# Edge loops of two graph layers: longer loop bodies, one comparison of a block reused for the next, and a comparison in fp32

## The chip, the cores and the metric

The kernel runs on one core of a Trainium2 chip. The metric is the device time of one execution in microseconds (us). TensorE (PE in the rows, PEld its weight loads) multiplies matrices, VectorE (DVE), ScalarE (ACT) and GpSimd (POOL) do the rest, and SyncE (SP) issues loads.

## What is computed

Four graph layers run one behind the other over 6250 nodes with 64 features and 206250 edges (100000 random pairs both ways, and a loop at each node), sorted by the destination `dst`. Each layer gathers something for the source of each edge and sums it per destination:

```python
edge_index = jnp.stack([src, dst])
x = layernorm(x + layer0(x, ...))   # two weighted sums over edges
x = layernorm(x + layer1(...))      # sum and maximum of edge features
x = layernorm(x + layer2(...))      # 4 Gaussian kernels: agg += segment_sum(gw[:, k] * xt[src, k], dst)
x = layernorm(x + layer3(...))      # messages: relu([x[src], x[dst], edge] @ W1.T + b1) @ W2.T + b2,
                                    # segment_sum(messages, dst), then a GRU cell
```

The change touches the loops over edges of layers 2 and 3.

## The kernel before

**Blocks.** The edges are cut into 51 blocks of 4096 (`NBK`), which are placed once, ahead of the layers, in a grid of 49 tiles of 128 node slots (`NT`), so that most edges of a block stand at the place of their source node. The rest of them, 9 x 128 rows of a block (`SC` = 9), is kept as a second list. A block's destinations lie in a window of 128 (`W`) nodes, those of its second list in groups of columns of 160 (`WS`). How many groups of columns a block may need is counted at run time (`n_windows`); for these inputs it is one, and there is one round over the blocks.

**How a sum is made.** The scatter to destinations is a matmul with a one-hot matrix: VectorE compares a row of numbers 0, 1, 2, ... with each edge's relative destination, and TensorE multiplies. A block takes 7 parts (`NS`) of 7 tiles (`SUB`), one comparison of 128 x 896 elements each (`g_hot` in layer 2, L2003; `m_hot` in layer 3, L2579). The second list has one-hots of its own, 128 x 9 x 160 in fp32 (`onehot`, made by `expand`, L2007 and L2600).

**Layer 2** (`layer2_edges`, L1880 on). For each part TensorE does 42 matmuls in bf16 (L1954), then a small one that turns a tile (L1961, once a block), at the end of the block 18 matmuls in fp32 for each group of columns (L1967, 36 instructions in the trace). VectorE makes for block n the products of the second list (L2019) and its one-hots, then in `hots` the comparisons for block n + 1, each as soon as TensorE has used that buffer, then it adds the block's window to the accumulators (L2034) and in the loop over groups of columns the second window (L2041), and expands again. GpSimd issues 9 gathers for a block (L1934), which wait for TensorE's progress (`hot_used`) so that they are spread over the block before.

**Layer 3** (`layer3_edges`, L2311 on). TensorE turns the edge features (L2429, L2430), makes the products of a part (L2439, L2443; ready: `pre_ready`), and three parts later reduces it (`reduce`, L2457 and L2460). In between, VectorE adds the source part (`add_src`, L2584), and with ScalarE splits the result into three bf16 parts (`take_high` L2590, `take_middle` L2596, after which `reduce` may start: `lo_ready`). At u == 1 VectorE also does `second`: cast the second list's destinations (L2606), subtract the group's first column (L2609), expand (L2600). At u == 5 it makes `mark` (L2620). At the block's end, in a loop over the groups of columns, it subtracts 160 from `rel` (L2665), waits for TensorE's window (L2508), adds it (L2667) and expands again, whether another group follows or not:

```python
with dve.Fori(0, count) as w:
    col = dve.value_load(cols[0:1, bass.ds(w, 1)], min_val=0, max_val=z.NP)
    v.tensor_scalar(rel[:, :], rel[:, :], -float(WS), None, ALU.add)
    dve.wait_ge(win_ready, before + w + 1)
    v.tensor_tensor(k.acc0[0:D, bass.ds(col, WS)], win_s[:, :], k.acc0[0:D, bass.ds(col, WS)], ALU.add)
    dve.drain()
    expand()
```

Then it adds the block's window (L2671), which sets `fast_ready`, and counts up `free`, after which SyncE loads for three blocks on. GpSimd issues 18 gathers a block in 9 pairs (L2407 and L2410, `m_from_src` and `m_from_dst`), of which six pairs first wait for a product of the block before (`pre_ready`).

**The loops.** Every engine runs the blocks through `over_rounds` (L656). Its body is written out for 6 blocks (two triples, since the buffers go by threes), and the loop turns 8 times; the last three blocks stand in line behind it.

## Time and profile before

| | |
|---|---|
| plain executions, median of 3 | 8629.86 us (8614.71 to 8640.16) |
| profiled execution | 8661.29 us, its span 8658.9 us |
| TensorE, weight loads | busy 60% and 50% of the span |
| VectorE | busy 53% |
| GpSimd | busy 50% |
| ScalarE | busy 18% |
| TensorE's granted clock over the span | 0.76 of full speed |

The profile shows one execution. The edge loop of layer 2 lies between about 5140 and 6545 us from the span's start, that of layer 3 between 6745 and 8575 us. In a row of a timeline stand start, duration, engine, line, operation, what it writes and reads, shapes and how many were merged; in square brackets how long the engine had been idle before it and what ended that ("issue": nothing that the profile shows; "remote": a semaphore whose setter it doesn't name). A name such as "DMA grid<-pay_d" as a releaser can stand for another use of the same semaphore number. Starts of matmuls are those of their issue, and their ends are modelled.

### The profile page before, as it was taken

The numbers are of one execution on the slowest core, as the hardware profiler recorded it, in microseconds if no ns is written. First come the engines' busy times: TensorE is split into PE (matmuls) and PEld (weight loads), VectorE is DVE, ScalarE is ACT, GpSimd is POOL, SyncE is SP. The second block draws the span as 40 slices with busy tenths as digits, with TensorE's granted clock in tenths as the row PEclk, the third lists the DMA queues.
The fourth block names the chain that finished last, engine by engine and source line by source line (L and its number), as shares of the span: only waits on it lengthen the run. The fifth ranks groups of instructions, "written<-read, shape, count | busy, mean of one in ns | idle before, by whom it ended". The sixth has DMA issues, their size and how long they took to land. (4 is left out here: it accounts for less than half of the span.)

```text
span 8658.9 us, 136636 instructions
## 1 busy us (share of the span) xinstructions
PE 5190.3 (60%) x47914; PEld 4348.2 (50%) x47915; DVE 4583.7 (53%) x8920; ACT 1567.8 (18%) x3149; POOL 4332.5 (50%) x4149
## 2 busy tenths in 40 slices
PE   2555555555555323253565448888886677777776
PEld 1334333433334222243554338888885566666665
DVE  4555555555555434353454554444445566666665
ACT  1111111111111100011111320000002333333332
POOL 3666666666666455513555613333330555555562
PEclk7776777667677666656766659999995789889897
DMA  3222222222222445521000301111111333333332
GB/s 110 88 86 82 82 87 87 87 84 87 87 87 73 84 91 100 98 24 55 22 21 21 119 16 21 21 21 21 21 20 19 121 97 96 93 97 100 95 95 52
DMA packets 379331, 599.64 MB, mean 69 GB/s; under 512 B 148462, under 2 KB 308192, under 8 KB 363811
## 3 DMA queue, kind: packets, MB, share of 16 engines
q1 hardware_dynamic: 235177, 472.07, 17.6%
q0 software_dynamic: 133216, 116.93, 6.6%
q8 instruction: 322, 5.28, 0.3%
q10 hardware_dynamic: 10454, 4.04, 0.2%
q14 instruction: 162, 1.33, 0.1%
HBM read 517.27 MB, written 213.23 MB: 84 GB/s over the span
## 5 line engine op out<-in xcount | busy, mean ns | idle before, releaser
L340 POOL DMA_INDIRECT pay_d<-row,place x1632 | 1728.3, 1059 | 1140.1 <-issue 531.1
L1954 PE MATMUL g_win<-g_hot,y_part 128*128 128x128 bf16 x14994 | 971.7, 227 | 263.5 <-issue 161.4
L443 PE MATMUL win<-onehot,val 128*128 128x128 f32 x4998 | 846.3, 336 | 409.5 <-ACT onehot L356 206.2
L1954 PEld LDWEIGHTS g_win<-g_hot,y_part 128*128 128x128 bf16 x14994 | 908.6, 102 | 319.2 <-issue 212.1
L443 PEld LDWEIGHTS win<-onehot,val 128*128 128x128 f32 x4998 | 768.1, 241 | 598.8 <-ACT onehot L356 349.9
L1934 POOL DMA_INDIRECT g_x<-xg_d,g_row x459 | 509.4, 1110 | 937.2 <-PE g_win L1954 723.1
L2407 POOL DMA_INDIRECT m_from_src<-from_src_d,m_row x459 | 507.1, 1105 | 633.4 <-PE m_pre L2443 402.6
L546 DVE TENSOR_TENSOR hot<-near_dve,drel 128x896 bf16<-128x896 bf16 x357 | 222.6, 624 | 1070.4 <-remote 772.7
L781 POOL DMA_INDIRECT r_x<-in_x,r_row x459 | 436.6, 951 | 448.4 <-PEq L821 254.3
L1278 POOL DMA_INDIRECT sorted_d<-s_row,s_place x459 | 444.6, 969 | 414.7 <-DVE s_place L1394 232.9
L2410 POOL DMA_INDIRECT m_from_dst<-from_dst_d,m_row x459 | 564.4, 1230 | 139.9 <-issue 135.9
L814 PE MATMUL r_win<-r_onehot,r_val 128*128 128x160 f32 x918 | 207.0, 403 | 614.3 <-DVEq L842 590.7
L413 PE MATMUL pair<-hot_hi,hot_lo 128*128 128x392 bf16 (+3 forms) x1632 | 296.8, 347 | 411.8 <-DVE hot_hi L484 411.8
L814 PEld LDWEIGHTS r_win<-r_onehot,r_val 128*128 128x128 f32 x918 | 193.1, 273 | 638.0 <-DVEq L842 606.4
L2439 PE MATMUL m_pre<-m_w_four,m_ea_t 96*128 96x192 f32 (+1 forms) x1428 | 477.9, 417 | 22.5 <-issue 21.9
L2443 PEld LDWEIGHTS m_pre<-m_q_win,m_hot_t 128*128 128x128 bf16 x7497 | 361.7, 104 | 214.3 <-issue 148.5
L413 PEld LDWEIGHTS pair<-hot_hi,hot_lo 128*128 128x128 bf16 x1632 | 200.7, 129 | 532.8 <-issue 236.2
L2443 PE MATMUL m_pre<-m_q_win,m_hot_t 128*128 128x64 bf16 x7497 | 402.4, 201 | 92.7 <-issue 88.5
L2584 DVE TENSOR_TENSOR m_hid<-m_pre,pq 128x448 f32<-128x448 f32 x357 | 222.3, 623 | 439.6 <-remote 220.7
L2003 DVE TENSOR_TENSOR g_hot<-iota_b,g_drel 128x896 bf16<-128x896 bf16 x364 | 214.3, 623 | 448.1 <-PE g_win L1954 256.3
L356 ACT ACTIVATE onehot<-hot 128x896 f32<-128x896 bf16 x357 | 334.5, 952 | 539.7 <-DVE hot L546 524.9
L2457 PE MATMUL m_win<-m_hot,m_parts 128*128 128x128 bf16 x2499 | 363.8, 234 | 110.7 <-issue 110.3
(452 smaller groups left out, 10694.8 us busy)
## 6 DMA issues: line engine op xcount, KB each, us to landing
m_hot_t<-drow_d SPq DMA_DIRECT2D x52, 1568.0 KB
scan_d<-in_none SPq DMA_DIRECT2D x51, 1034.2 KB
lo_row<-lo_d SPq DMA_DIRECT2D x51, 1024.0 KB
m_grid<-pay_d SPq DMA_DIRECT2D x52, 882.0 KB
pay_d<-in_fill SPq DMA_DIRECT2D x51, 882.0 KB
grid<-pay_d SPq DMA_DIRECT2D x51, 882.0 KB
pay_d<-in_fill SPq DMA_DIRECT2D x51, 648.0 KB
row<-in_pay SPq DMA_DIRECT2D x51, 576.0 KB
```

Source lines behind the costliest of these rows:

```text
L340: pool.indirect_dma_start(a["pay_d"][:, :], bass.IndirectOffsetOnAxis(ap=place[j][:, c:c + 1], axis=0), row[j][:, c, :], None).then_inc(ro ...
L413: last = mm(pair[h][:, q, c * NT:BK * NT].rearrange("p (n s) -> p n s", s=NT), hot_lo[:, e, :], hot_hi[:, e, 0:NT].unsqueeze(1).to_broadca ...
L443: last = mm(win[:, :], val[u % 2][:, s, :], onehot[u % 2][:, s, :], start=(u == 0 and s == 0), stop=(u == NS - 1 and s == SUB - 1))
L781: pool.indirect_dma_start(xs[j][:, c, :], None, a["x"][:, :], bass.IndirectOffsetOnAxis(ap=row[j][:, c, AT_SRC:AT_SRC + 1].bitcast(i32), a ...
L814: mm(win[j][:, :], val[j][:, c, :], onehot[j][:, c, :], start=(c == 0), stop=(c == SC - 1))
L1278: pool.indirect_dma_start(a["sorted_d"][:, :], bass.IndirectOffsetOnAxis(ap=place[j][:, c:c + 1], axis=0), row[j][:, c, :], None).then_inc ...
L1934: pool.indirect_dma_start(xs[j][:, c, :], None, a["xg_d"][:, :], bass.IndirectOffsetOnAxis(ap=row[j][:, c, AT_SRC:AT_SRC + 1].bitcast(i32) ...
L1954: last = mm(win[:, h, 0:W], k.y[q][:, t, h * P:(h + 1) * P], hot[u][:, s, :], start=(t == 0 and q == 0), stop=(t == NT - 1 and q == 2))
L2407: pool.indirect_dma_start(ps_x[j][:, c, :], None, a["from_src_d"][:, :], bass.IndirectOffsetOnAxis(ap=row[j][:, c, AT_SRC:AT_SRC + 1].bitc ...
L2410: pool.indirect_dma_start(qs_x[j][:, c, :], None, a["from_dst_d"][:, :], bass.IndirectOffsetOnAxis(ap=row[j][:, c, AT_DST:AT_DST + 1].bitc ...
L2439: mm(out[:, first * D:(first + size) * D], ea_t[u % 2][0:size * F, o:o + P], w_four[0:size * F, 0:size * D], start=True, stop=False)
L2443: last = mm(out[:, s * D:(s + 1) * D], hot_t[j][:, (u * SUB + s) * P:(u * SUB + s + 1) * P], q_win[j][:, q * D:(q + 1) * D], start=False, ...
```

## The change

Five things are done. `over_rounds` gets a parameter `turn`, the triples in a turn: layers 2 and 3 pass 8, so that the body is written out for 24 blocks and turns twice, with three blocks in line behind it; other callers keep 2. In layer 2 `hots` compares fp32 numbers with each edge's relative destination (one bf16 element, broadcast) and no longer pairs of bf16; the result is bf16 as before. In layer 3 the first expansion of a block is gone: `second` (at u == 1 of block n) copies the prepared `rel_next` to slot 0 of `rel`, and prepares `rel_next` for block n + 1 (`relative`); the loop over groups writes slot w + 1, then overwrites slot `count` with `rel_next`, so that its last expansion makes the one-hots of the next block, and TensorE waits for one expansion less a block. Around that: the first block's one-hots are made ahead of the loop, `k.group` has one column more, and SyncE loads one set of rows more at the end. Last, some tiles are allocated in a scope that ends before layer 2.

```diff
-def over_rounds(eng, z, k, body):
+def over_rounds(eng, z, k, body, turn=2):
     thirds = z.NBK // 3
     rounds = n_rounds(eng, k)
     with eng.Fori(0, rounds) as r:
-        with eng.Fori(0, thirds // 2) as i:
-            for h in range(2):
+        with eng.Fori(0, thirds // turn) as i:
+            for h in range(turn):
                 for j in range(3):
-                    body(r * z.NBK + i * 6 + (h * 3 + j), r * thirds + i * 2 + h, i * 6 + (h * 3 + j), j, r)
-        for m in range(thirds - thirds % 2, thirds):
+                    body(r * z.NBK + i * (3 * turn) + (h * 3 + j), r * thirds + i * turn + h, i * (3 * turn) + (h * 3 + j), j, r)
+        for m in range(thirds - thirds % turn, thirds):
...
@@ layer2_edges, hots
-                        v.tensor_tensor(hot[u][:, :, :].rearrange("p s (w q) -> p s w q", q=2), by_twos(k.iota_b[:, :], SUB),
-                                        two_each(twos(drel[j][:, u * SUB:(u + 1) * SUB]), W), ALU.is_equal).then_inc(hot_ready, 1)
+                        v.tensor_tensor(hot[u][:, :, :], k.iota[:, :].unsqueeze(1).to_broadcast([P, SUB, W]),
+                                        twos(drel[j][:, u * SUB:(u + 1) * SUB])[:, :, 0:1].to_broadcast([P, SUB, W]),
+                                        ALU.is_equal).then_inc(hot_ready, 1)
...
@@ layer3_edges
-        rel = sb("m_rel", [P, SC])
+        rel = sb("m_rel", [P, MW + 1, SC])
+        rel_next = sb("m_rel_next", [P, SC])
...
-                        pe.wait_ge(onehot_ready, before + n + w + 1)
+                        pe.wait_ge(onehot_ready, before + w + 1)
...
-                def second(n, m, b, j):
+                def relative(n, m, j):
                     dve.wait_ge(row_in[j], m * 16 + 16)
                     v.tensor_copy(dst_f[:, :], row[j][:, :, AT_DST].bitcast(i32))
+                    dve.drain()
+                    v.tensor_scalar(rel_next[:, :], dst_f[:, :], k.group[:, at(n)], None, ALU.subtract)
+
+                def second(n, nxt, nm, nj):
+                    v.tensor_copy(rel[:, 0, :], rel_next[:, :])
                     v.tensor_scalar(cols[:, :], k.shift[:, :], k.group[0:1, at(n)], float(z.NP), ALU.add, ALU.min)
                     dve.drain()
-                    v.tensor_scalar(rel[:, :], dst_f[:, :], k.group[:, at(n)], None, ALU.subtract)
-                    dve.drain()
-                    expand()
+                    relative(nxt, nm, nj)
...
+                relative(0, 0, 0)
+                dve.drain()
+                v.tensor_copy(rel[:, 0, :], rel_next[:, :])
+                dve.drain()
+                expand(rel[:, 0:1, :])
...
-                            second(n, m, b, j)
+                            second(n, nxt, m + (j == 2), nj)
...
-                        v.tensor_scalar(rel[:, :], rel[:, :], -float(WS), None, ALU.add)
+                        v.tensor_scalar(rel[:, bass.ds(w + 1, 1), :], rel[:, bass.ds(w, 1), :], -float(WS), None, ALU.add)
+                        dve.drain()
+                        v.tensor_copy(rel[:, bass.ds(count, 1), :], rel_next[:, :].unsqueeze(1))
                         dve.wait_ge(win_ready, before + w + 1)
                         v.tensor_tensor(k.acc0[0:D, bass.ds(col, WS)], win_s[:, :], k.acc0[0:D, bass.ds(col, WS)], ALU.add)
                         dve.drain()
-                        expand()
+                        expand(rel[:, bass.ds(w + 1, 1), :])
```

## Rows read from the trace of the kernel before

**Rows 1.** Busy times by stretch: layer 2's, then layer 3's edge loop.
```profile
5140.00:6545.00 1405.00, 1230.02 (x16931) 1169.01 (x16931) 607.46 (x1078) 17.32 (x55) 509.38 (x459) 0.94 0.12 21
6745.00:8575.00 1830.00, 1397.76 (x16020) 1139.13 (x16021) 1197.17 (x2040) 678.66 (x1684) 1069.37 (x916) 0.88 0.31 94
```
**Rows 2.** Timelines: first instructions behind a turn, layer 2 (two), layer 3.
```profile
6296.79 2.53 PE L1954 MATMUL g_win<-g_hot,y_part 128*128 128x128 bf16 x22 [5.67 <-issue]
...
5647.03 0.17 DVE L2013 CAST g_dst_f<-g_row 128x9 f32<-128x9 int32 x1 [5.26 <-issue]
...
8251.11 0.32 PE L2429 MATMUL m_ea_ps<-ident,m_ea 128*128 128x128 f32 x1 [3.94 <-issue]
```
**Rows 3.** Timelines of VectorE and TensorE in one block of layer 3.
```profile
7583.08 1.66 DVE L2600 TENSOR_TENSOR m_onehot<-m_near_dve,m_rel 128x1440 f32<-128x1440 f32 x1
...
7585.99 0.62 DVE L2596 TENSOR_TENSOR m_parts<-m_left,m_parts 128x448 bf16<-128x448 f32 x1
...
7586.71 0.22 PE L2457 MATMUL m_win<-m_hot,m_parts 128*128 128x128 bf16 x1 [1.62 <-issue]
...
7603.89 1.30 PE L2508 MATMUL m_win_s<-m_onehot,m_hid_s 128*64 128x160 f32 x8
```
**Rows 4.** Timelines of GpSimd, VectorE, TensorE in three blocks of layer 3.
```profile
7597.75 0.94 POOL L2410 DMA_INDIRECT m_from_dst<-from_dst_d,m_row  x1 [0.30 <-issue]
...
7599.96 0.62 DVE L2584 TENSOR_TENSOR m_hid<-m_pre,pq 128x448 f32<-128x448 f32 x1 [2.17 <-remote]
...
7953.07 0.94 POOL L2410 DMA_INDIRECT m_from_dst<-from_dst_d,m_row  x1 [0.30 <-issue]
...
7952.55 0.74 PE L2439 MATMUL m_pre<-m_w_four,m_ea_t 128*128 128x256 f32 x1
...
7955.29 0.62 DVE L2584 TENSOR_TENSOR m_hid<-m_pre,pq 128x448 f32<-128x448 f32 x1 [2.92 <-remote]
...
7886.22 0.63 DVE L2584 TENSOR_TENSOR m_hid<-m_pre,pq 128x448 f32<-128x448 f32 x1 [0.20 <-issue]
...
7888.49 2.52 POOL L2410 DMA_INDIRECT m_from_dst<-from_dst_d,m_row  x1 [0.30 <-issue]
```
**Rows 5.** Timelines of VectorE, GpSimd and TensorE in one block of layer 2.
```profile
5612.57 0.56 DVE L2041 TENSOR_TENSOR acc<-g_win_s,acc 128x160 f32 x2 [2.92 <-PE g_win_s L1967]
...
5622.45 2.23 DVE L2003 TENSOR_TENSOR g_hot<-iota_b,g_drel 128x896 bf16<-128x896 bf16 x4 [0.69 <-PE g_win L1954]
...
5619.29 1.54 POOL L1934 DMA_INDIRECT g_x<-xg_d,g_row  x1 [1.52 <-PE g_win L1954]
...
5622.87 1.02 POOL L1934 DMA_INDIRECT g_x<-xg_d,g_row  x1 [0.31 <-issue]
5624.20 1.30 POOL L1934 DMA_INDIRECT g_x<-xg_d,g_row  x1 [0.30 <-issue]
...
5622.20 3.93 PE L1954 MATMUL g_win<-g_hot,y_part 128*128 128x128 bf16 x63
5626.44 0.51 PE L1954 MATMUL g_win<-g_hot,y_part 128*128 128x128 bf16 x6 [0.30 <-issue]
```
**Rows 6.** One instruction a block: all 51, then stretches of five; duration, first and last start.
```profile
L1961 PE MATMUL g_drel_t<-ident_b,g_drel x51: 239/240/241, 5164.4 to 6518.7; 128*49 128x128 bf16 x51
...
L1961 PE MATMUL g_drel_t<-ident_b,g_drel x5: 239/239/240, 6168.6 to 6273.9; 128*49 128x128 bf16 x5
...
L2671 DVE TENSOR_TENSOR acc<-m_win,acc x51: 291/292/294, 6799.2 to 8560.6; 128x128 f32 x51
...
L2671 DVE TENSOR_TENSOR acc<-m_win,acc x5: 291/292/294, 7255.7 to 7391.8; 128x128 f32 x5
...
L2671 DVE TENSOR_TENSOR acc<-m_win,acc x5: 291/292/293, 7472.0 to 7610.7; 128x128 f32 x5
```
**Rows 7.** Groups by line in layer 2's loop: count | busy us, mean ns | idle.
```profile
L2003 DVE TENSOR_TENSOR g_hot<-iota_b,g_drel 128x896 bf16<-128x896 bf16 x364 | 214.3, 623 | 448.1 <-PE g_win L1954 256.3 <-DMA grid<-pay_d 182.8 <-DMA g_drel<-drel_d 5.3
L2007 DVE TENSOR_TENSOR g_onehot<-steps_ws,g_rel 128x1440 f32<-128x1440 f32 x102 | 169.2, 1659 | 8.2
```

More of the change, by code:

```diff
@@ L1969, in body @@
                         last.then_inc(win_ready, 1)
[L1971 removed]
+                over_rounds(pe, z, k, body, turn=8)
             @block.scalar
@@ L2044, in body @@
                     dve.sem_inc(free, 1)
-                over_rounds(dve, z, k, body)
+                over_rounds(dve, z, k, body, turn=8)
                 dve.drain()
@@ L2388, in body @@
                     load_grid(n, b)
-                over_rounds(sp, z, k, body)
+                over_rounds(sp, z, k, body, turn=8)
                 rounds = n_rounds(sp, k)
@@ L2511, in body @@
                         reduce(n, u)
-                over_rounds(pe, z, k, body)
+                over_rounds(pe, z, k, body, turn=8)
             @block.scalar
@@ L2563, in body @@
                     middle(n, NS - 1)
-                over_rounds(act, z, k, body)
+                over_rounds(act, z, k, body, turn=8)
             @block.vector
@@ L2672, in body @@
                     dve.sem_inc(free, 1)
-                over_rounds(dve, z, k, body)
+                over_rounds(dve, z, k, body, turn=8)
                 dve.drain()
@@ L2830, in build @@
         k.acc0 = sb("acc0", [P, z.NC])
-        k.ones = sb("ones", [P, P])
         k.ident = sb("ident", [P, P])
-        k.before = sb("before", [P, P])
-        k.after = sb("after", [P, P])
         k.iota = sb("iota", [P, P])
@@ L2873, in build @@
                 sb, ps, sem = make(nc, early)
+                k.ones = sb("ones", [P, P])
+                k.before = sb("before", [P, P])
+                k.after = sb("after", [P, P])
+                k.base = sb("base", [P, z.NBK])
+                k.cell_at = sb("cell_at", [P, z.NBK])
+                k.cnt_sec = sb("cnt_sec", [P, z.NT])
+                k.cnt_src = sb("cnt_src", [P, z.NT])
+                k.cnt_grid = sb("cnt_grid", [P, z.NT])
                 k.total = sb("total", [P, z.NT * F])
```

25 lines of the change are left out of this document (11 added, 14 removed).

## The prediction, made before the changed kernel was run

> **What bounds the kernel now.** I first took the busy shares of the two stretches that the change touches [rows 1]. The edge loop of layer 2 takes 1405 us with TensorE busy for 1230 of them. That of layer 3 takes 1830 us, with TensorE busy for 1398, VectorE for 1197 and GpSimd for 1069. So layer 2 runs at TensorE's pace, and layer 3 has no engine that is always busy: there I looked for the waits, block by block, in the timelines.
>
> Three things show. *First, the turns of the loops.* Every sixth block TensorE stands for 4 to 6 us at the same place, the first matmul of the loop body, and VectorE as long (5.67 and 5.26 us in layer 2, 3.94 in layer 3) [rows 2]. The releaser is given as "issue": nothing that the profile knows holds it. There are 7 such gaps in each layer, as many as the present loop branches back (8 turns of 6 blocks, then 3 blocks in line), and none at a seam of two blocks inside the body. *Second, a wait in layer 3.* In the middle of nearly every block TensorE stands for 1.6 us before its first reduction matmul and starts 0.10 us after VectorE ends `take_middle` (7585.99 + 0.62 = 7586.61, then 7586.71) [rows 3]. VectorE is late there because it has just spent 1.66 us on the one-hots of `second`. The row names "issue", but VectorE is the releaser. *Third, the gathers.* In both layers GpSimd issues gathers back to back, and TensorE falters behind them [rows 4, 5]. In layer 3, VectorE gets the sixth product of a block 1.27 us after GpSimd ends its 12th gather (7598.69, then 7599.96).
>
> **The change, part by part.** The profiled execution spans 8658.9 us and took 8661.3 us; the median of the plain runs is 8629.9, so 31.4 less. I sum against 8661.3 and carry the result over by that difference.
>
> *Turns of 24 blocks.* 17 triples are now 2 turns of 8 and one triple left over: one branch back for each layer, so 6 go in each. The price of one is read from the steps. Layer 2: 50 steps from block to block take 1354.3 us, and four without a branch 105.3, so 26.33 each [rows 6]. (1354.3 - 50 x 26.33) / 7 = 5.4 us; the bare gap is 5.67 [rows 2]; I take 5.6. Layer 3: 1761.4 us in 50 steps; two stretches of four give 34.03 and 34.68 each [rows 6], mean 34.35, so (1761.4 - 50 x 34.35) / 7 = 6.3, with 3.9 and 8.6 by either one alone, and a gap of 3.94 [rows 2]. I take 6.3: what was in flight on the other engines starts anew too, so more than the gap is lost. Gain: 6 x 5.6 + 6 x 6.3 = 71 us, bounds 55 (6 x 5.26 + 6 x 3.9) and 86 (6 x 5.67 + 6 x 8.6). Nothing hides it: all engines branch at once, and TensorE is the one that stands. Longer bodies on ACT, GpSimd and SyncE may make their one remaining branch dearer. No row shows theirs alone; by VectorE's 5.26 [rows 2] it is 0 to 5 us a layer. I take 0, since these three wait for TensorE most of the time.
>
> *Layer 3, the one-hots.* `second` (at u == 1) loses the comparison (1.66 us and the drain behind it, some 0.15), and gains a 9-element copy (0.17 us, as the cast in rows 2) and one drain, some 0.3 us; the cast and the subtraction stay, for the next block. So `take_middle` comes about 1.5 us earlier. TensorE's wait of 1.62 us shrinks to about 0.1 [rows 3]. What is late next is the gathers' burst. It starts when the second product is ready, which the edit does not move, and then runs at GpSimd's own pace. Compare two blocks [rows 4]: in the first, VectorE's sixth `add_src` (L2584) comes 1.27 us after the 12th gather's end; in the second, TensorE is already at the seventh product (L2439) at 7952.55, yet the sixth `add_src` comes at 7955.29, again 1.28 us after the gather (7954.01). Being ahead did not bring the signal forward. Behind it VectorE's own chain (`mark` and two more rounds) fills the rest of the block. So of 1.5 us I let 0.3 through: gathers that overlap fewer two-input operations of VectorE. 51 x 0.3 = 15 us. Bounds: 0 and 1.5 a block, 0 to 77 us.
>
> The expansion at a block's end, whose result nobody used, now makes the next block's one-hots. TensorE takes them up in its window matmuls (7603.89 in this block), 20 us behind even the comparison that is removed (7583.08) [rows 3]: no wait. The copy and a drain added at that place put 0.3 to 0.4 us before `fast_ready`, which TensorE needs only at its next first reduction, and before `free`, for loads three blocks ahead. The rows that `second` now reads a block earlier are loaded up to three blocks ahead. The one added load stands in SyncE's queue ahead of the last, unused grid load, with the rest of the block before it. The new start of the layer (about 2.5 us of VectorE, by the same operations) lies beside the first loads and products. All of these at 0; without that cover the start would cost 2.5 us once. The moves of tiles cost nothing at run time.
>
> *Layer 2, comparisons in fp32.* 896 elements took 623 ns. The comparison that is all fp32 takes 1659 ns for 1440 [rows 7], and the fp32 `add_src` 620 for 448 [rows 4], that is 1.047 ns an element, so 620 + 448 x 1.047 = 1089 ns: +0.47 us, 3.3 us a block, on an engine that is busy for 607 of 1405 us. The buffers are filled a block ahead, and before the accumulation at the block's end VectorE waits 2.92 us for TensorE [rows 5]: hidden, as work. But it lengthens gathers. One takes 0.94 us alone [rows 4], 1.54 over the fp32 product and comparison, 1.02 and 1.30 over the bf16 comparisons [rows 5]. Four comparisons in a row take 4 x 1.0 us and no longer 2.23, lie over three gathers and no longer two, and cost 3 x 0.6 - 0.08 - 0.36 = 1.4 us of the burst. TensorE runs at full pace over the stretched ones (63 matmuls in 3.93 us) and falters behind (6 from 5626.44, then a gap) [rows 5], so a longer burst need not be a longer block. Bounds: +1.4 us a block, and -0.9 if a third of the faltering went: TensorE is idle (1405 - 1230) / 51 = 3.4 us a block [rows 1], of which the turns are 7 x 5.6 / 51 = 0.8. I take +0.3, the nearer to nothing since most of the idle time stays as it is: 51 x 0.3 = +15 us, bounds -46 to +71.
>
> Here the row comes first: the gathers over VectorE's two-input fp32 operations are 0.6 us longer. The Trainium skill, "GPSIMD Engine Reference", section Key points, says why: GpSimd shares its SBUF interfaces with VectorE, and contends with instructions that have two SBUF inputs. Both forms of the comparison have two, so by that rule the burden grows with their time, which speaks against this part of the change. Read at its hardest, the rule gives case (c) below; by the row, where TensorE keeps its pace over the stretched gathers, it gives the sum's +0.3.
>
> Sum: 8661.3 - 71 - 15 + 15 = 8590 for a profiled execution, 8559 for the median.
>
> **The rivals.** (a) *The 1.5 us arrive.* Then 77 and not 15: 8497. For it: TensorE does stand for VectorE in the row. Against: the two blocks of rows 4. Chance 0.17. (b) *The sixth product slips in ahead of the gathers.* One block does it: its `add_src` came at 7886.22, when the 12th gather had not yet begun (7888.49) [rows 4], so it was spared two gathers and the 1.27 us behind them, 2 x (0.94 + 0.30) + 1.27 = 3.75 us. If TensorE 1.5 us earlier did this in 40 blocks, 150 us in place of 15: 8424. Chance 0.05. (c) *The fp32 burst passes on whole*, +1.4 us a block: 8559 + 51 x 1.1 = 8615. Chance 0.10. (d) *The turns bring nothing*, since the gaps come with the amount of code and not with branches; the change would then not do what its loops are for: 8630. Against it: every gap sits at a branch, and the three blocks in line behind the loop show none. Chance 0.04. (e) *Slower.* The gathers wait for all of the added comparison time, 3.3 us a block, and the end of the burst holds TensorE as in layer 3: 8559 + 51 x 3.0 = 8712. It turns the sign once more than 0.3 + (8630 - 8559) / 51 = 1.7 us a block reach TensorE. Against it: the bf16 comparisons, 2.23 us in a row, lengthened two gathers by 0.08 and 0.36. Chance 0.05.
>
> **How the numbers follow.** The likeliest case has 0.59. About 0.3% (26 us) is what a measurement of this kernel can tell from no change, so faster means under 8604, slower over 8656. The likeliest case and (a), (b) are faster: 0.81. Same: (c) and (d): 0.14. Slower: (e): 0.05. The likeliest case alone spans 8515 to 8600: its terms by their bounds, not all at one end. The range takes in (a) with the same margin and (c), and leaves out (b), (d), (e): 8460 to 8616.
>
> **What the profile after would show.** One gap of about 5 us in each layer, 24 blocks from its start, and steps of 26.6 and 34.1 us between; if there are seven, (d). In layer 3, `take_middle` of a block's first part some 1.5 us earlier against the block's start and no gap of 1.6 us before L2457's counterpart; if the step is then 32.9 us, (a); if it stays near 34.1 and the sixth `add_src` still comes about 1.3 us after the 12th gather, mine. In layer 2, comparisons of 1.09 us and gathers of 1.4 to 1.5 us under them; a step near 27.7 us means (c), 29.5 means (e). Wrong I would be above all if TensorE's faltering hangs on something else than the gathers, so that either step moves on its own.

## The result, and the profile after

The changed kernel takes 8356 us (median of 4 runs, 8338 to 8374) where the kernel before, on the same chip, takes 8635 (4 runs): a ratio of 0.9677, interval 0.9643 to 0.9711, 279 us less. The forecast was 8559 us, with a range from 8460 to 8616. The sign was right; the time lies 104 us below the range. On two other chips the same kernel took 8377 us, a ratio of 0.9727 each time (e6 and e14 below), 236 and 233 us less than before: also below the range, but the size of the gain differs by some 40 us from chip to chip.

The stretches of the two loops in the profile after (window; length, then busy us of TensorE, its weight loads, VectorE, ScalarE, GpSimd; granted clock, DMA share, GB/s):

```profile
5117.00:6267.00 1150.00, 1121.89 (x16881) 1101.62 (x16881) 768.55 (x1078) 17.32 (x55) 576.13 (x459) 0.99 0.13 25
6482.00:8250.00 1768.00, 1355.43 (x15981) 1119.29 (x15978) 1129.88 (x2091) 672.72 (x1680) 1017.16 (x911) 0.90 0.31 96
```

One instruction of each block, all 51, as in [rows 6] (min/median/max duration in ns; first and last start):

```profile
L1962 PE MATMUL g_drel_t<-ident_b,g_drel x51: 239/240/304, 5131.9 to 6247.8; 128*49 128x128 bf16 x51
...
L2686 DVE TENSOR_TENSOR acc<-m_win,acc x51: 291/292/294, 6528.4 to 8243.8; 128x128 f32 x51
```

So the profiled time (8344.8 us, 316.5 less than before's profiled 8661.3) went here: layer 2's 50 steps 1354.3 to 1115.9, 238 less; layer 3's 1761.4 to 1715.4, 46 less; and the first of these rows stands 32.5 us earlier, 25 of them ahead of layer 2's first matmul, in layers that the change doesn't touch, and no more than differs between kernels that are alike up to there (e5 to e8, all on one chip, have it between 5163 and 5200 us). **Nearly the whole surprise is layer 2**, which I had at 19 us less (34 for the turns, 15 lost to the fp32 comparison). There TensorE is now busy for 1122 of 1150 us at a granted clock of 0.99; it was 1230 of 1405 at 0.94 [rows 1]. Busy time itself fell, for two reasons. Where TensorE falters, matmuls that start a few at a time count longer (5 in 0.44 us, below, against 126 in 7.21). And the granted clock is at the lower of its two levels for 137 us of layer 2's 50 steps before and for 23 after. If everything runs at half pace there, that is at most (137 - 23) / 2 = 57 of the 238 us, an estimate. Before, a step without a branch takes 25.1 us on average where the clock stays up and about 26.7 where it falls for 3.4 us.

One block of layer 2 after, in the timelines of GpSimd, VectorE and TensorE, to be held against [rows 5]:

```profile
5493.49 7.21 PE L1955 MATMUL g_win<-g_hot,y_part 128*128 128x128 bf16 x126
5500.53 5.11 PE L1968 MATMUL g_win_s<-g_onehot,g_val 128*128 128x160 f32 x36
...
5493.36 6.12 DVE L2004 TENSOR_TENSOR g_hot<-iota,g_drel 128x896 bf16<-128x896 f32 x6 [0.23 <-issue]
...
5494.25 1.02 POOL L1935 DMA_INDIRECT g_x<-xg_d,g_row  x1 [0.30 <-issue]
5495.57 1.70 POOL L1935 DMA_INDIRECT g_x<-xg_d,g_row  x1 [0.30 <-issue]
5497.58 1.70 POOL L1935 DMA_INDIRECT g_x<-xg_d,g_row  x1 [0.30 <-issue]
5499.58 0.94 POOL L1935 DMA_INDIRECT g_x<-xg_d,g_row  x1 [0.30 <-issue]
5500.83 0.94 POOL L1935 DMA_INDIRECT g_x<-xg_d,g_row  x1 [0.30 <-issue]
```

And more of the same place of a block before, where [rows 5] ended:

```profile
5627.20 0.44 PE L1954 MATMUL g_win<-g_hot,y_part 128*128 128x128 bf16 x5 [0.26 <-issue]
5627.97 0.33 PE L1954 MATMUL g_win<-g_hot,y_part 128*128 128x128 bf16 x3 [0.32 <-issue]
5628.70 0.45 PE L1954 MATMUL g_win<-g_hot,y_part 128*128 128x128 bf16 x5 [0.41 <-issue]
5630.13 1.15 PE L1954 MATMUL g_win<-g_hot,y_part 128*128 128x128 bf16 x11 [0.98 <-issue]
...
5625.80 0.94 POOL L1934 DMA_INDIRECT g_x<-xg_d,g_row  x1 [0.30 <-issue]
5627.05 0.94 POOL L1934 DMA_INDIRECT g_x<-xg_d,g_row  x1 [0.30 <-issue]
5628.30 0.94 POOL L1934 DMA_INDIRECT g_x<-xg_d,g_row  x1 [0.30 <-issue]
```

Before, the last gathers of a block start 1.25 us apart and TensorE issues three to five matmuls every 0.75 us or so. After, they start 1.32, 2.01, 2.00 and 1.25 us apart, 126 matmuls run in 7.21 us without a gap, and a step is 21.8 us (21.6 to 22.0), except the loop's first (33.6), the one with the branch (28.0) and the one behind it (27.3). What lengthens the gathers is VectorE's fp32 comparison, six in a row, which I had priced rightly (the rows by line: 1087 ns each, forecast 1089; a gather 1255 ns on average, 1110 before, so 9 x 0.145 = 1.3 us of the burst, forecast 1.4).

The one branch left in each loop is where it was foretold, 24 blocks from the start; in layer 2:

```profile
5663.35 3.85 PE L1955 MATMUL g_win<-g_hot,y_part 128*128 128x128 bf16 x40 [4.79 <-issue]
...
5666.31 0.17 DVE L2015 CAST g_dst_f<-g_row 128x9 f32<-128x9 int32 x1 [5.31 <-issue]
```

The Trainium skill, "Runtime: NRT & Kernel Launch", section Instruction fetch mechanics, says that a taken branch whose target isn't held yet waits for a fetch. These rows agree that the branch stalls, for 4.8 and 5.3 us; that it is a fetch they do not show.

### The profile page after: what moved, and what is told of

Same layout as the page of the kernel before. It is cut to its first block and busy times, and to the rows that moved or that the text cites. A ratio compares the mean times of both kernels' runs of the same rounds, so it can differ in the third digit from the quotient of the medians.

```text
span 8343.2 us, 136715 instructions
## 1 busy us (share of the span) xinstructions
PE 5058.7 (61%) x47914; PEld 4272.0 (51%) x47915; DVE 4679.7 (56%) x8976; ACT 1562.3 (19%) x3149; POOL 4352.3 (52%) x4149
## 5 line engine op out<-in xcount | busy, mean ns | idle before, releaser
L1955 PE MATMUL g_win<-g_hot,y_part 128*128 128x128 bf16 x14994 | 872.3, 220 | 121.1 <-DVE g_hot L2004 100.3
L1955 PEld LDWEIGHTS g_win<-g_hot,y_part 128*128 128x128 bf16 x14994 | 850.2, 98 | 136.0 <-DVE g_hot L2004 100.5
L1935 POOL DMA_INDIRECT g_x<-xg_d,g_row x459 | 576.1, 1255 | 631.6 <-PE g_win L1955 428.0
L2412 POOL DMA_INDIRECT m_from_src<-from_src_d,m_row x459 | 539.7, 1176 | 634.5 <-PE m_pre L2448 398.2
L2415 POOL DMA_INDIRECT m_from_dst<-from_dst_d,m_row x459 | 485.0, 1057 | 139.9 <-issue 139.3
L2444 PE MATMUL m_pre<-m_w_four,m_ea_t 96*128 96x192 f32 (+1 forms) x1428 | 478.7, 418 | 18.8 <-issue 18.3
L2004 DVE TENSOR_TENSOR g_hot<-iota,g_drel 128x896 bf16<-128x896 f32 x364 | 375.2, 1087 | 130.2 <-PE g_win L1955 113.7
L2465 PE MATMUL m_win<-m_hot,m_parts 128*128 128x128 bf16 x2499 | 339.7, 229 | 82.2 <-DVE m_parts L2601 63.5
```

The source lines that it names most:

```text
L1935: pool.indirect_dma_start(xs[j][:, c, :], None, a["xg_d"][:, :], bass.IndirectOffsetOnAxis(ap=row[j][:, c, AT_SRC:AT_SRC + 1].bitcast(i32) ...
L1955: last = mm(win[:, h, 0:W], k.y[q][:, t, h * P:(h + 1) * P], hot[u][:, s, :], start=(t == 0 and q == 0), stop=(t == NT - 1 and q == 2))
L2412: pool.indirect_dma_start(ps_x[j][:, c, :], None, a["from_src_d"][:, :], bass.IndirectOffsetOnAxis(ap=row[j][:, c, AT_SRC:AT_SRC + 1].bitc ...
L2415: pool.indirect_dma_start(qs_x[j][:, c, :], None, a["from_dst_d"][:, :], bass.IndirectOffsetOnAxis(ap=row[j][:, c, AT_DST:AT_DST + 1].bitc ...
L2444: mm(out[:, first * D:(first + size) * D], ea_t[u % 2][0:size * F, o:o + P], w_four[0:size * F, 0:size * D], start=True, stop=False)
```

## The experiments

The theory after reading the trace, **A**: TensorE falters where GpSimd issues gathers back to back, from about the third on, and whatever pulls them apart takes the faltering away. The rivals: **B**, the longer loop bodies did it; **C**, the form of the comparison matters to TensorE by itself. All steps below are means of the 50 in one profile (last start less first, by 50). "Ahead" counts, of 49 blocks of layer 3, those in which VectorE's sixth `add_src` starts over 1 us before GpSimd ends its 12th gather, case (b) of the prediction. "Low clock" is for how many us of layer 3's 50 steps TensorE's granted clock was at the lower of its two levels, by the trace's clock records.

| kernel | us | of before | layer 2 step | layer 3 step | ahead | low clock |
|---|---|---|---|---|---|---|
| before | 8635 | 1 | 27.1 | 35.2 | 2 | 399 |
| changed | 8356 | 0.968 | 22.3 | 34.3 | 23 | 338 |
| e1, fp32 alone | 8477 | 0.981 | 23.5 | 35.1 | 1 | 375 |
| e2, turns alone | 8569 | 0.991 | 26.3 | 33.9 | 13 | 276 |
| e3, one-hots alone | 8623 | 0.998 | 27.1 | 34.7 | 28 | 365 |
| e4, pauses | 8513 | 0.983 | 24.3 | 35.1 | 0 | 379 |
| e5, changed, old one-hots | 8334 | 0.968 | 22.0 | 33.1 | 19 | 239 |
| e6, changed | 8377 | 0.973 | 22.1 | 34.2 | 10 | 352 |
| e7, changed, fp32 in layer 3 | 8338 | 0.968 | 22.1 | 33.8 | 39 | 215 |
| e8, changed, pauses in layer 3 | 8497 | 0.987 | 22.2 | 36.7 | 49 | 498 |
| e9, narrow rows (one execution) | 8599 | | 26.3 | 33.8 | 19 | 270 |
| e10, half the rows (one execution) | 8621 | | 26.9 | 33.9 | 20 | 273 |
| e11, bf16 twice (one execution) | 8560 | | 26.3 | 33.9 | 19 | 283 |
| e12, changed, spare comparison | 8283 | 0.961 | 22.1 | 32.1 | 42 | 133 |
| e13, e5 and e7 together | 8311 | 0.965 | 22.2 | 33.0 | 48 | 109 |
| e14, changed | 8377 | 0.973 | 22.2 | 34.1 | 10 | 355 |

Layer 3's order varies by itself too: e9 to e11 have layer 3 as before, and yet 19 and 20 blocks with the product ahead. Nor does the count fix the step: e3 has 28 blocks ahead and steps of 34.7 us, e2 has 13 and 33.9. The kernel before took 8647 us beside e1 to e4, 8614 beside e5 to e8, 8603 beside e9 and e10, and 8611 beside e11 to e14. Four more runs fell on chips of another kind and stand further below.

### Each part alone

e1 has only the comparison of layer 2 changed:

```
-  v.tensor_tensor(hot[u]..., by_twos(k.iota_b[:, :], SUB), two_each(twos(drel[j]...), W), ALU.is_equal)
+  v.tensor_tensor(hot[u][:, :, :], k.iota[:, :].unsqueeze(1)..., twos(drel[j]...)[:, :, 0:1]..., ALU.is_equal)
```

> The kernel before with only the comparison of layer 2 in fp32 (128x896 with an fp32 iota and fp32 numbers), no longer loop bodies, layer 3 as before. Theory A (TensorE falters when GpSimd issues three or more gathers 1.2 us apart, 0.94 us and a pause of 0.30; the longer comparison pulls two of them apart to 2.0 us): -190 to -210 us, layer 2 steps of 21.9 us between branches, 28 us at one. Theory B (the longer loop bodies took the faltering away): within 20 us of before, steps of 26.3 us.

e2 has only the loops changed:

```
-  over_rounds(pe, z, k, body)
+  over_rounds(pe, z, k, body, turn=8)
```

> The kernel before with only the loops of layers 2 and 3 turning every 24 blocks. The prediction's term and theory A: -60 to -75 us (six branches fewer in each layer at 5.6 and 6.3 us), layer 2 steps of 26.3 us, faltering as before. Theory B: -240 us and more, steps of 21.9 us.

e3 is the changed kernel with both of these undone:

> The changed kernel with loops that turn every 6 blocks and the bf16 comparison in layer 2: what is left is layer 3's one-hots. The prediction's term: -15 us, 0.3 us a block. From the changed kernel's trace (layer 3 is 46 us shorter, of which the turns should be 38): -5 to -15 us. Rival (a), the 1.5 us arrive: -77 us. In the trace VectorE's sixth product should come before the end of the 12th gather in some 20 of 50 blocks, as in the changed kernel, where it was 2 of 50 before.

Measured against before on one chip: e1 -170 us, 20 less than A had said: its steps with a branch take 28 to 30 us and those behind one 24 to 27 (ratio 0.9811, 0.9788 to 0.9834), e2 -78 (0.9909, 0.9892 to 0.9926), e3 -24 (0.9976, 0.9961 to 0.9991), more than the 5 to 15 us expected and far less than the rival's 77. Their loops, one instruction a block as above; the first is e1, the next two e2, the last e3:

```profile
L1961 PE MATMUL g_drel_t<-ident_b,g_drel x51: 239/240/304, 5159.4 to 6332.7; 128*49 128x128 bf16 x51
```
```profile
L1961 PE MATMUL g_drel_t<-ident_b,g_drel x51: 239/240/241, 5159.5 to 6475.4; 128*49 128x128 bf16 x51
...
L2671 DVE TENSOR_TENSOR acc<-m_win,acc x51: 291/292/294, 6755.4 to 8448.1; 128x128 f32 x51
```
```profile
L2685 DVE TENSOR_TENSOR acc<-m_win,acc x51: 291/292/294, 6789.1 to 8524.4; 128x128 f32 x51
```

B falls, and so far A and C both stand: with the long bodies alone layer 2 keeps its faltering, 1315.9 us in 50 steps; with the fp32 comparison alone it is 1173.3, 181 us less. The branch was priced well in layer 2: (1354.3 - 1315.9) / 6 = 6.4 us each where the forecast took 5.6. In layer 3 it is (1761.4 - 1692.7) / 6 = 11.4 where it took 6.3; not all of that is the branch, since the sixth product gets ahead in 13 blocks and no longer in 2, and a block in which it does took 31.6 us there against 34.9. TensorE's gap at a branch of layer 3 is only 3.9 to 4.8 us before. Of the 69 us most goes with the clock: the time at its lower level falls from 399 to 276 us.

### What pulls gathers apart, and what about them matters

e4 keeps the bf16 comparisons and lets GpSimd pause:

```
                         ).then_inc(x_in[j], 16)
+                        if c >= 5:
+                            pool.memset(pause[:, :], 0.0)
+                            pool.drain()
```

> The kernel before with bf16 comparisons in layer 2 as they were, and GpSimd filling a scratch tile of 128x512 after each of a block's last four gathers, which puts them 0.5 us or more further apart. Theory A (what counts is the spacing of gathers, by whatever means): the faltering goes, layer 2 steps of 22 to 23 us between branches, -150 to -210 us. Theory C (the comparison's own form or length matters for TensorE, not the gathers' spacing): steps of 26.3 us or more, 0 to +50 us.

One of its blocks (the last gathers, and TensorE beside them):

```profile
5692.41 0.94 POOL L1935 DMA_INDIRECT g_x<-xg_d,g_row  x1 [0.30 <-issue]
5693.34 0.55 POOL L1939 MEMSET g_pause<- 128x512 f32 x1
5696.00 0.95 POOL L1935 DMA_INDIRECT g_x<-xg_d,g_row  x1 [2.10 <-issue]
...
5689.95 7.36 PE L1958 MATMUL g_win<-g_hot,y_part 128*128 128x128 bf16 x126
```

-134 us (ratio 0.9829, 0.9804 to 0.9854), a little short of the 150 to 210 that A had said. The pause is longer than I meant, 2.1 us of drain behind the 0.55, so that in some blocks the last gathers slide into the next block, where they bunch up with its own. Of the 50 steps 17 take 21.8 to 22.1 us, 15 take 22.9 to 24.5, and the others, those with a branch among them, more. **C falls** as the whole cause: the comparison is the old one, and 126 matmuls run in 7.36 us.

Then, what of a gather does it? e9 fetches 68 bytes for each of 128 rows and not 272, e10 fetches 64 rows and not 128:

```
-  pool.indirect_dma_start(xs[j][:, c, :], None, a["xg_d"][:, :], ...
+  pool.indirect_dma_start(xs[j][:, c, 0:17], None, a["xg_d"][:, :].rearrange("n (f w) -> (n f) w", w=17), ...   (e9)
+  pool.indirect_dma_start(xs[j][0:P // 2, c, :], None, a["xg_d"][:, :], ...                                     (e10)
```

> The kernel before with layer 2's gathers fetching 68 bytes for each of 128 rows and not 272 (of each row's 68 numbers 17 are fetched, from other places, so layer 2's second part is computed from other numbers). If the faltering comes from the bytes that the gathers move: it shrinks, steps of 22 to 24 us. If it comes from GpSimd's making of 128 descriptors each 1.2 us: nothing changes, steps of 26.3 us and gathers of 0.94 us.

> The kernel before with layer 2's gathers fetching 64 rows and not 128 (half of each tile stays zero, so half of layer 2's second part is left out). If the faltering comes from the descriptors, by their number: half as many in the same time, it goes or shrinks, steps of 22 to 24 us, unless the gathers become shorter too and keep the same rate. If it hangs on GpSimd's being in a gather at all: as before, 26.3 us.

One execution each, and neither computes the kernel's result: e9 leaves out three quarters of each fetched row, e10 half of the rows. Layer 2's steps are 26.3 and 26.9 us, against 27.1 before and 22 to 23.5 where the faltering is gone or mostly gone. A gather takes 0.95 us with a quarter of the bytes and 0.91 with half the rows. So the bytes can be a small part of it at most (0.8 us a block), and the number of rows is not it. It goes with GpSimd being in one gather after another.

e11 asks whether any load of VectorE would pull them apart:

```
+  v.tensor_tensor(spare[:, :, :]..., by_twos(k.iota_b[:, :], SUB), two_each(...), ALU.is_equal)
+  dve.drain()
   v.tensor_tensor(hot[u]..., by_twos(k.iota_b[:, :], SUB), two_each(...), ALU.is_equal).then_inc(hot_ready, 1)
```

> The kernel before with each bf16 comparison of layer 2 preceded by the same comparison into a scratch tile: 2 x 0.62 us of VectorE where the fp32 form has 1.09. If the time that VectorE works over the gathers is what pulls them apart, whatever its form: steps near 21.9 us and -170 us. If only fp32 operands do it (the gathers over bf16 comparisons took 1.02 and 1.30 us, those over fp32 ones 1.7 and 2.1): gathers stay 1.2 to 1.6 us apart, faltering as before or a little later, steps of 25 to 27 us, -60 to +50 us.

```profile
5402.86 0.94 POOL L1935 DMA_INDIRECT g_x<-xg_d,g_row  x1 [0.30 <-issue]
5404.11 0.94 POOL L1935 DMA_INDIRECT g_x<-xg_d,g_row  x1 [0.30 <-issue]
5405.36 0.94 POOL L1935 DMA_INDIRECT g_x<-xg_d,g_row  x1 [0.30 <-issue]
...
5400.62 4.81 PE L1955 MATMUL g_win<-g_hot,y_part 128*128 128x128 bf16 x83
5405.66 0.38 PE L1955 MATMUL g_win<-g_hot,y_part 128*128 128x128 bf16 x4 [0.23 <-issue]
5407.07 0.38 PE L1955 MATMUL g_win<-g_hot,y_part 128*128 128x128 bf16 x4 [1.03 <-issue]
```

The second answer holds, with one execution: a gather takes 1117 ns on average (1110 before), and TensorE falters nearly as before (steps of 26.3 us), here from the start of the third short gather in a row (5405.36). VectorE works as long over the gathers as with the fp32 form, but in bf16 it hardly lengthens them. The Trainium skill, "GPSIMD Engine Reference", section Key points, names VectorE's instructions with two SBUF inputs among those that GpSimd contends with. By that rule e11 should have lengthened the gathers as the fp32 form does; the measurement says that the form decides. And the lengthening, which I had weighed as a cost, was the gain.

### Layer 3: why the one-hots cost time in the full change

e5 is the changed kernel with layer 3's old one-hots, e6 the changed kernel itself; e7 adds the fp32 comparison to layer 3, e8 this to each pair of its gathers:

```
+                        pool.memset(pause[:, :], 0.0).then_inc(paused, 1)
+                        pool.wait_ge(paused, n * SC + (c + 1))
```

> The kernel before with the fp32 comparison in layer 2 and the loops of 24 blocks, layer 3's one-hots as before: the changed kernel less one part. If the parts add up: the 78 us of the turns alone and the 170 us of the comparison alone, and some 15 to 20 us more, since the trace of the changed kernel has 1116 us for layer 2 where 1354 - 38 - 181 = 1135 would be the sum: -245 to -270 us, and 15 to 25 us behind the changed kernel (the one-hots alone brought 24). Rival (the one-hots bring nothing once the turns are long, since layer 3 took 1715 us in the changed kernel and 1693 with the turns alone): as fast as the changed kernel or up to 20 us faster.

> The changed kernel itself, beside the others on one chip, as their measure: 0.967 to 0.970 of before, -260 to -285 us; layer 3 between 1690 and 1720 us in its profile, if that stage varies from execution to execution.

> The changed kernel with layer 3's seven comparisons a block in fp32 too, fp32 numbers from SBUF and not bf16 ones from PSUM. Theory A (gathers 1.2 us apart make TensorE falter; longer two-input operations of VectorE pull them apart): fewer falterings in layer 3, 1 to 3 us a block, -50 to -150 us against the changed kernel. Rival: VectorE, the releaser of TensorE in layer 3, carries 7 x 0.47 = 3.3 us more a block, and layer 3 gets longer: +50 to +150 us.

> The changed kernel with GpSimd filling a scratch tile of 128x512 (0.54 us) after every pair of layer 3's gathers and waiting for it, 9 times a block: some 0.7 us more between pairs, 6 us more of GpSimd's time a block (22 becomes 29 of 34 us). Theory A: the faltering shrinks or goes, -50 to -150 us against the changed kernel, steps of 31 to 33 us. Rival (layer 3 is held by VectorE's chain or by late gathers, not by the faltering): 0 to +50 us.

e5 was 43 us *faster* than the changed kernel (0.9677, 0.9659 to 0.9696, against 0.9727, 0.9707 to 0.9747): my expectation failed, and its rival had the sign, but allowed for 20 us only. The part that was worth 24 us by itself costs 43 beside the long turns and layer 2's new comparison. e6 itself came out at 0.9727 where I expected 0.967 to 0.970. e7 was 40 us faster than the changed kernel, the sign that A foretold and less than its 50 to 150; in the profiles layer 3 holds 24 of them. e8 was 120 us slower: behind each pair GpSimd stood for 0.8 to 1.1 us more than the memset's 0.54, twice the pause I wanted, a pair with its pause took 3.5 to 5.7 us and nine took 36.7; GpSimd became the bound, and that says nothing on A.

The comparison that the one-hots' edit removes is 1.66 us of VectorE in fp32 with two inputs, in the middle of the block. To see whether its absence is what costs, e12 puts a useless one in its place, in the changed kernel:

```
                             second(n, nxt, m + (j == 2), nj)
+                            for h in range(2):
+                                v.tensor_tensor(spare[:, :, :], steps[:, 0:WS // 2]..., rel[:, 0:1, :]..., ALU.is_equal)
+                                dve.drain()
```

> The changed kernel with a spare comparison where layer 3's one-hots used to be made (two of 128x720 fp32 into a scratch tile that nobody reads, some 1.7 us a block): pure extra work. Theory (the removed comparison had pulled three gathers apart there, and without it TensorE falters earlier and longer): as fast as the kernel with the old one-hots, 30 to 50 us faster than the changed kernel; VectorE's sixth product earlier by about 1 us a block, GpSimd's gathers 0.5 us a block longer. Rival (the loss comes from something else of that part, the copy and drain before the block's last sum or the moved tiles): as slow as the changed kernel or slower, 0 to +60 us.

> The changed kernel with layer 3's old one-hots (43 us faster than the changed kernel) and with fp32 comparisons in layer 3 (40 us faster alone). If each spaces out other gathers, they add up in part: 50 to 80 us faster than the changed kernel, the fastest kernel of the study. If VectorE becomes the bound in layer 3: slower than either alone.

> The changed kernel itself, as the measure of the others on the same chip: 0.967 to 0.973 of before.

e12, e13 and e14 in this order, the spare work first:

```profile
L2664 DVE TENSOR_TENSOR m_spare<-m_near_dve,m_rel x102: 898/904/909, 6562.7 to 8175.5; 128x720 bf16<-128x720 f32 x102
...
L2692 DVE TENSOR_TENSOR acc<-m_win,acc x51: 291/292/294, 6590.8 to 8196.7; 128x128 f32 x51
```
```profile
L2673 DVE TENSOR_TENSOR acc<-m_win,acc x51: 291/292/294, 6564.5 to 8214.0; 128x128 f32 x51
```
```profile
L2686 DVE TENSOR_TENSOR acc<-m_win,acc x51: 291/292/294, 6582.0 to 8286.8; 128x128 f32 x51
```

**1.8 us of useless work a block makes the kernel 94 us faster**: 8283 us (0.9606, 0.9573 to 0.9638), the fastest of the study, with layer 3 at 1605.9 us and not 1704.9. e13 has 8311 us, 67 less than the changed kernel: within the 50 to 80 expected, though not the fastest. So it is the time that the comparison took which is missed, not the copy, the drain or the moved tiles. One mark that I had named did not show: the gathers are not 0.5 us a block longer (20.5 us of GpSimd in both). What the traces show is order. Averaged over 49 blocks and counted from a block's last sum, the fifth `add_src` starts at 16.7 us in e14 and at 16.6 in e12, GpSimd's ninth gather at 17.0 and 17.6, the sixth `add_src` at 22.5 and 20.4. With the spare work the row of gathers starts 0.6 us later and the sixth product gets ahead of its end in 42 blocks; without it, in 10.

The traces show one thing more, which none of these theories named: TensorE's granted clock. Layer 3's 50 steps in e14, e12, e6 and e5 (columns as for the stretches above):

```profile
6582.00:8286.80 1704.80, 1349.24 (x15696) 1098.77 (x15694) 1110.35 (x2050) 664.77 (x1648) 998.34 (x883) 0.90 0.31 98
6590.80:8196.70 1605.90, 1240.84 (x15698) 1034.93 (x15697) 1191.86 (x2150) 658.65 (x1648) 1003.92 (x882) 0.96 0.33 104
6575.50:8287.30 1711.80, 1346.98 (x15698) 1102.88 (x15698) 1108.40 (x2051) 664.38 (x1650) 991.33 (x882) 0.90 0.31 97
6578.40:8231.40 1653.00, 1288.76 (x15698) 1066.42 (x15698) 1172.50 (x2001) 663.70 (x1650) 1018.30 (x882) 0.93 0.32 101
```

TensorE's idle time is no less in the faster kernels (356 us in e14, 365 in e12; 365 in e6, 364 in e5). What falls is its busy time, by 108 and 58 us, while the layer gets shorter by 99 and 59 us. The time at the lower level of the clock falls by 355 - 133 = 222 us and 352 - 239 = 113 us, and half of that is 111 and 56. So nearly all that the spare comparison and the old one-hots win in layer 3 is accounted for by the clock. It stays up throughout 2 of e14's 50 steps and 27 of e12's, and on chips of this kind every such step in these traces, where the order was counted, is one with the sixth product ahead. Being ahead is not enough (e3: 28 blocks ahead, 365 us at the lower level). That the order keeps the clock up is the reading that fits; no run changed the order and nothing else on such a chip, so it is not shown.

## Two kinds of chip

e15 was meant to test that order: in the changed kernel GpSimd waits with the ninth gather for the sixth product and not for the fifth. e16 has the same wait with the old one-hots.

```
-  pool.wait_ge(pre_ready, n * NS + (c // 3 * 2 + c % 3 + 3))
+  pool.wait_ge(pre_ready, n * NS + (c // 3 * 2 + c % 3 + 3 + (c == 4)))
```

> The changed kernel, where in layer 3 GpSimd waits with a block's ninth gather (c == 4) for TensorE's sixth product and not for the fifth: one number in a wait. Theory (the sixth product falls into the long row of gathers; in the changed kernel the row starts 0.6 us earlier against it than with the spare comparison): the sixth product gets ahead in nearly all of 49 blocks, steps of 31 to 32 us, 80 to 130 us faster than the changed kernel (0.957 to 0.963 of before). Rival (the row of gathers then starts some 3 us later, ends later, and what it feeds, or the next block's start, waits instead): -20 to +80 us against the changed kernel.

> The same wait in the kernel with the old one-hots of layer 3 (43 us faster than the changed kernel). Theory: with the order settled, the 1.7 us of VectorE that the old one-hots take in the middle of a block are cost again: this kernel is as fast as the one with the new one-hots and that wait, or up to 40 us slower. Rival (the old one-hots help by spacing gathers, whatever the order): it is 20 to 60 us faster than that one.

Both ran on a chip on which the kernel before takes 7009 us, and so did the last two, the changed kernel (e17) and e15's kernel (e18), on another one with 7014:

> The changed kernel itself. On a chip where the kernel before takes 8600 us: 0.967 to 0.973 of before, steps of 21.8 us in layer 2 and 34.2 us in layer 3. On a chip where it takes 7008 us and TensorE does not falter: the turns (some 65 us) and layer 3's one-hots remain, the fp32 comparison is worth nothing, -60 to -140 us, steps of 21.6 us in layer 2 and 25 to 26 us in layer 3.

> The changed kernel, where in layer 3 GpSimd waits with a block's ninth gather for TensorE's sixth product and not for the fifth. On a chip with the faltering, theory (the order of the sixth product and the row of gathers decides): 80 to 130 us faster than the changed kernel, steps of 31 to 32 us; rival (the row ends later and holds something else): -20 to +80 us against it. On a chip without: within 20 us of the changed kernel.

| kernel | us | of before | layer 2 step | layer 3 step | ahead | low clock |
|---|---|---|---|---|---|---|
| e15, ninth gather later | 6871 | 0.9805 (0.9789 to 0.9822) | 21.9 | 25.6 | 49 | 7 |
| e16, the same, old one-hots | 6932 | 0.9888 (0.9872 to 0.9905) | 21.9 | 26.9 | 49 | 14 |
| e17, changed | 6875 | 0.9805 (0.9789 to 0.9822) | 21.9 | 25.7 | 49 | 7 |
| e18, as e15 | 6875 | 0.9805 (0.9789 to 0.9822) | 21.9 | 25.7 | 49 | 10 |

The same kernel with the same row of gathers in layer 3, first on the chip of e14, then on that of e17:

```profile
6870.51 0.94 POOL L2412 DMA_INDIRECT m_from_src<-from_src_d,m_row  x1 [0.30 <-issue]
6871.76 0.94 POOL L2415 DMA_INDIRECT m_from_dst<-from_dst_d,m_row  x1 [0.30 <-issue]
...
6871.42 0.28 PE L2448 MATMUL m_pre<-m_q_win,m_hot_t 128*128 128x64 bf16 x4
6872.20 0.31 PE L2448 MATMUL m_pre<-m_q_win,m_hot_t 128*128 128x64 bf16 x5 [0.50 <-issue]
6873.65 0.25 PE L2448 MATMUL m_pre<-m_q_win,m_hot_t 128*128 128x64 bf16 x3 [1.14 <-issue]
6875.07 0.48 PE L2444 MATMUL m_pre<-m_w_four,m_ea_t 96*128 96x192 f32 x2 [1.18 <-issue]
```
```profile
5701.85 0.94 POOL L2415 DMA_INDIRECT m_from_dst<-from_dst_d,m_row  x1 [0.30 <-issue]
5703.09 0.94 POOL L2412 DMA_INDIRECT m_from_src<-from_src_d,m_row  x1 [0.30 <-issue]
5704.34 0.94 POOL L2415 DMA_INDIRECT m_from_dst<-from_dst_d,m_row  x1 [0.30 <-issue]
...
5704.33 0.51 PE L2448 MATMUL m_pre<-m_q_win,m_hot_t 128*128 128x64 bf16 x12
5704.68 0.57 PE L2444 MATMUL m_pre<-m_w_four,m_ea_t 96*128 96x192 f32 x2
5705.09 0.43 PE L2448 MATMUL m_pre<-m_q_win,m_hot_t 128*128 128x64 bf16 x9
```

On the second chip these rows of gathers leave TensorE's pace alone (the kernel before has no trace from there; what follows is the changed kernel's). Over the fourth and later short gathers in a row, it starts 15.7 weight loads on average in the 1.25 us from a gather's start (264 gathers), and 4.0 on the chip of e14 (37). GpSimd's short gathers take 0.94 us on both. The clock stays up too; layer 3's 50 steps in e17:

```profile
5491.70:6777.70 1286.00, 1138.81 (x15689) 985.01 (x15685) 1095.29 (x2051) 654.73 (x1646) 987.66 (x890) 1.00 0.41 130
```

That is 419 us less than in e14, of which the clock explains at most (355 - 7) / 2 = 174. So the faltering belongs to GpSimd's gathers *and* to the chip. How else the two kinds of chip differ is open: layer 2's loop starts 1062 us earlier in e17 than in e14, in layers that were not studied here. What the change wins there is 139 us, of which the one-hots are 61 (e16 less e15, 1.2 us a block: near my case (a), and more than the 0 to 40 us that I had expected of e16). That leaves 78 for the turns and the fp32 comparison together. It is what the turns won alone on the other kind (e2), so the comparison may be worth about nothing here; but part of e2's gain was the clock, and neither was run alone on such a chip, so this split is not shown.

The later ninth gather is worth nothing there (e17 and e18 agree). Whether it would do on the first kind of chip what the spare comparison did stays untested.

## Why the prediction was wrong, step by step

**The turns: right.** -71 forecast with bounds of 55 and 86, -78 measured (e2). One gap in each layer, 4.8 us in layer 2 and 5.7 in layer 3, where the prediction put it. That the total fits is in part luck: of the 78 us layer 3 brought more than the forecast's 38 (69 in the profiles), most of it by the clock.

**Layer 3's one-hots: right alone, wrong in the sum.** Forecast -15 us (bounds 0 and -77); -24 alone (e3), +43 in the full change (e5 against e6), -61 where TensorE doesn't falter (e16 against e15). The mechanics came in part: with the one-hots alone the first `take_middle` starts 0.9 us earlier and not 1.5 (10.5 to 9.6 us after a block's start, on average; 8.9 in the full change, where the turns add theirs), and TensorE's wait before its first reduction shrinks from 1.6 to 0.7 us. The step that failed is "what is late next is the gathers' burst ... at GpSimd's own pace", with the sixth `add_src` pinned 1.27 us behind the 12th gather. The 1.27 us [rows 4] were not a property of the gathers: they varied with how TensorE fared in them. Before, the distance lies between 1.2 and 1.35 us in 18 of 50 blocks, in the changed kernel in none, and in 23 of 49 the product is ahead. My case (b) had this mechanism and its size (3.75 us; 34.9 - 31.6 = 3.3 in e2), at a chance of 0.05, and held it to be started by an earlier TensorE; by e12 and e14 it goes as well with when the gathers start, so an edit can undo it too. And the sum has no term for TensorE's granted clock, which stood in [rows 1] at 0.88: half of the change in the time at its lower level is 56 of the 59 us by which layer 3 is longer in e6 than in e5. No bound of mine reached a cost. That layer 3 as a whole came out near the forecast (46 us less, forecast 38 + 15) is luck: the turns brought 69 there by themselves, and the one-hots took part of it back.

**Layer 2's comparison: the term that broke the sum.** +15 us forecast, -170 measured (e1), bounds +71 and -46. The comparison's time and the gathers' lengthening were right to 0.1 us. Wrong was the upside. I had seen in [rows 5] that TensorE keeps its pace over stretched gathers and falters behind short ones, and then allowed for "a third of the faltering", a number with no row behind it. And I took the idle time (1405 - 1230) for all that could be won, though busy time held slow matmuls too. The row to use was the one at full pace: [rows 5] has 63 matmuls in 3.93 us, so 294 of them and the block's 36 window matmuls (5.11 us, before as after) take 18.3 + 5.1 = 23.4 us by that row, or 16.8 + 5.1 = 22 by the pace after (126 in 7.21), against steps of 26.3: an upside of 3 to 4 us a block, 150 to 220 us, and not 46. Nearly all of it came, since the stretch breaks up the row of short gathers at a block's end. The clock is a part of it, and again had no term: in e1 it is at the lower level for 63 us of layer 2's steps and not 137, at most 37 of the 181 us.

**The last sentence** named what would make it wrong, that "TensorE's faltering hangs on something else than the gathers". It hangs on them, but on how closely they follow each other, not on how many there are.

**The Trainium skill's rule** on contention says nothing of a block's time; it was my reading that it speaks against this part. For the fp32 form the traces agree with it (gathers of 1.70 us under these comparisons), for the bf16 form they hardly do (e11), and a longer gather was what TensorE needed.

Still open: what in GpSimd's gather keeps TensorE from its instructions (all these gaps are "issue", no semaphore is late); why from about the third; why on some chips only; and what in layer 3 decides in which blocks the clock falls.

## What to carry to other kernels

When an engine falters beside another's work, price the upside by a block at full pace, not by its idle time, give "the faltering goes" a case of its own, and compare the granted clock of the stretches: where busy time falls and idle time doesn't, the clock may be what changed. Look at the spacing of GpSimd's gathers: where three or more stand 1.25 us apart beside bf16 matmuls, anything that pulls them apart, even useless work, may pay, and removing an operation there may cost. Before keeping such a repair, measure on several chips: on the second kind the one-hots are worth 61 us where they cost 43 on the first, and the rest of the change 78 where e5 has 280.

## What the runs showed of the hardware that I had not expected

- A chip may let TensorE falter beside GpSimd's gathers or not: 8603 to 8647 us and 7009 to 7014 us for the same kernel before, with short gathers at 0.94 us on both (in the changed kernel; the kernel before was not profiled on the second kind).
- Where it does, two short gathers in a row do little (e11: TensorE starts some 9 weight loads each half microsecond through rows of two), and in rows of four it is down to 0.6 half a microsecond after the third's start, from 9 at the row's start; a memset of 0.54 us and a drain between them prevents it (e4).
- An fp32 comparison of VectorE with two SBUF inputs lengthens a gather from 0.94 to 1.7 us (99 of 459 gathers in the changed kernel, none before; those of 2.1 us, under the one-hots and the comparison behind them, are 36 before and 37 after). The bf16 form, twice and so 1.24 us long, left as many at 0.94 as before (302 and 293 of 459; e11).
- At a branch back TensorE stands for 4.6 to 5.7 us in layer 2 and 3.9 to 5.7 in layer 3; a branch less was worth 6.4 us in layer 2. In the changed kernel the block behind it is long too, 27.3 us against 21.8, and on the second kind of chip it is not (21.6, e17).
- The granted clock can decide more than idle time does: in layer 3 the spare comparison's 99 us came with as much idle time of TensorE as before, and a granted clock of 0.96 for 0.90 (e12, e14).
